# Storing the turned queries, keys and values of the head attention as the transposes yield them

## The chip, the core and the metric

The kernel runs on one core of a Trainium2 chip. The metric is the time of one execution on the device, in microseconds (us). The core's engines run side by side, each with its own queue of instructions, and meet through semaphores: PE (TensorE, the matrix products), DVE (VectorE), ACT (ScalarE), POOL (GpSimd) and SP (which here only issues DMA transfers). PEld is the loading of weights into PE, which overlaps with its products.

## The reference, cut to what matters

For each of 32 sequences of 256 tokens with 256 features, a linear ("performer") attention over a context runs first. Its result is added to `x`, and then a block with its own norms follows: an attention among the heads of each single token, and eight experts.

```python
x = x + tanh(g_xattn[0]) * xattn(layernorm(x), ctx_1024, ctx_1024, random_features)
x = x + tanh(g_ffn[0]) * ffn(layernorm(x), ...)

def ffn(x, ...):                                    # H = 16 heads of HD = 16 features
    h = rmsnorm(x, gamma1)
    q = (h @ Wq + bq).reshape(b, t, H, HD)
    kv = ((h @ Wdown + bdown) @ Wup + bup).reshape(b, t, H, 2 * HD)
    k, v = split(kv, 2, axis=-1)
    att = softmax(einsum('bthd,btgd->bthg', q, k) / sqrt(HD), axis=-1)
    out = einsum('bthg,btgd->bthd', att, v).reshape(b, t, D)
    x = x + (out @ Wo + bo)
    h2 = rmsnorm(x, gamma2)
    gate = softmax(h2 @ Wg + bg, axis=-1)
    return x + einsum('btd,edf,bte->btf', h2, We, gate)
```

The change concerns `q`, `k` and `v` of that attention among heads.

## The kernel before

One batch is one sequence: 256 tokens, as two tiles of 128 partitions by 256 features. Every engine has its list of steps; a step (`v_bd_`, `m00_`, `av0_`) is a small function that takes a batch number, waits for the steps that it needs, issues its instructions and signals its end. The order of the steps is written out by hand in each engine's part. A prologue brings in the first batches step by step, then a loop runs the function `slot(n)` 25 times (n = 6 to 30), and an epilogue drains the last batches. One slot works on several batches at once: features of the linear attention for batch n + 2, its scores and sums for n + 1, the norm of the second block for n, the head attention for n - 1, its output product for n - 2, the experts for n - 3.

The head attention of a batch goes like this. `bqq_`, `bkv0_` and `bkv1_` on DVE write queries, keys and values with their biases into `qkv`, tokens on the partitions. `q_t_`, `k_t_` and `v_t_` (lines 1519, 1612, 1581) turn blocks of 32 x 32 on DVE, so that the 16 features of a head lie on partitions and the tokens along the free side: `q_t` and `k_t` hold 32 tokens (n) by 16 heads, `v_t` 32 tokens by 16 features. Each of these tiles is stored with the token outside and the 16 inside, while the transpose yields 16 runs of 32 tokens; its destination is therefore written with a stride of 16 elements. Then the tiles are spread to block-diagonal operands: on ACT `q_bd_` makes two copies of `q_t` (line 899) and `k_bd_` four of `k_t` (line 932), each times a 0/1 column; on POOL `v_bd_` makes four of `v_t` (line 465). PE's `s_` multiplies `k_bd` with `q_bd` in 32 small products, DVE and ACT do the softmax, and PE's `pv_` multiplies the weights with `v_bd`.

Two other chains matter for the order. PE's `o_` (the product with `Wo`) for batch n - 2 is followed by `y2_` on DVE (line 1576), and that by `z0_` on POOL (lines 449 and 451). And the linear attention for batch n + 1 has masks on POOL: ACT copies scores to `att` (`x000_`, `x001_`, `x010_`, `x011_`), POOL blanks the future tokens (`m01_` line 473, `m00_` line 482), and PE's `av0_` (line 2348) multiplies with them. In POOL's slot these stand as `z0_(n - 2)`, `x1_(n)`, `v_bd_(n - 1)`, `m01_(n + 1)`, `m00_(n + 1)`. In PE's slot, `o_` stands ahead of six groups of score products (`X00_` to `X10_`), then come `av0_(n + 1)`, `s_(n - 1)`, `av1_(n + 1)`, `mm00_`, `mm01_`. Another POOL step, `d_v_` (line 420), copies 256 elements into `down_v`, reading every fourth.

Of the kernel before, what the change touches and what calls it, by code (L numbers as in the profile page):

```python
# [79 lines left out]
def build(nc, x_d, ctx_d, gx_d, gf_d, rf_d, g1_d, wq_d, bq_d, wdn_d, bdn_d, wup_d, bup_d,  # L80
          wo_d, bo_d, g2_d, wg_d, bg_d, we_d, out_d):
    ctx = ExitStack()
    with ctx:
# [57 lines left out]
        q_t, k_t, v_t = sb("q_t", [P, 32, H]), sb("k_t", [P, 32, H]), sb("v_t", [P, 32, HD])  # L141
# [33 lines left out]
        with ExitStack() as early:  # L175
# [18 lines left out]
            signal("once_pe0", "first_turned first_all most_turned stab_all"),  # L194
            signal("pe0", "fk fq X00 Y1"),
            signal("pe1", "X01 X11 av3 nt_t"),
            signal("pe2", "Y0 X10"),
            signal("pe3", "av0 av1"),
            signal("pe4", "hn_t qq s"),
            signal("pe5", "dn kv0"),  # L200
            signal("pe6", "kv1 pv"),
            signal("pe7", "o_tr o h2_t0"),
            signal("pe8", "h2_t1 mm1g mm10 mm11"),
            signal("pe9", "mm0g mm12"),
            signal("pe10", "mm00 mm01 mm03"),
            signal("pe11", "mm02 mm13"),
# [17 lines left out]
            signal("once_act0", "alpha we_hi3 wg_hi"),  # L224
            signal("keys_act0", "square"),
            signal("act0", "h_hi"),
            signal("act1", "k_hi h_t ek2"),
            signal("act2", "xn ek3 eq3"),
            signal("act3", "ek0 x000 x001 x100"),
            signal("act4", "q_hi eq0 x010"),  # L230
            signal("act5", "ek1 eq2 x011 x110 x101"),
            signal("act6", "eq1 nt0 nt1"),
            signal("act7", "x111"),
            signal("act8", "hn ht_hi d_hi q_bd"),
            signal("act9", "k_bd p_bd ot_hi"),
            signal("act10", "y"),
            signal("act11", "sq h2n h2_hi1"),
            signal("act12", "h2_hi0 gexp"),
            signal("once_pool0", "one_tri zero_id ident f_scale f_hi f_lo"),
            signal("pool0", "k_lo pk2"),  # L240
            signal("pool1", "rstd q_r"),
            signal("pool2", "q_lo pk0 m01 m10 m11"),
            signal("pool3", "pq3 m00"),
            signal("pool4", "v1"),
            signal("pool5", "pq1"),
            signal("pool6", "x1 r_f g_r"),
            signal("pool7", "d_v v_bd"),
            signal("pool8", "yb"),
            signal("pool9", "o_n ms_e r2"),
            signal("pool10", "z_y z0"),  # L250
# [41 lines left out]
        def _(sp):  # L292
            @per_batch
            def store_(b):
                if b >= 0:
                    sp.wait_ge(*at("a03", b))
                sp.wait_ge(*at("a13", b))
                sp.dma_start(rows(out_d, b), z[b % 2][:, :, :]).then_inc(*store.up(b))
# [91 lines left out]
            for n in range(6, NB + -1):  # L390
                slot(n)
# [6 lines left out]
            sp.wait_ge(*store.at(NB - 1))  # L398

        @block.gpsimd  # L400
        def _(pool):
# [6 lines left out]
            def pk0_(b):  # L408
                if b >= 0:
                    pool.wait_ge(*at("ek0", b))  # L410
# [43 lines left out]
            def x1_(b):  # L454
                if b >= 0:
# [21 lines left out]
            def m00_(b):  # L477
                if b >= 0:
                    pool.wait_ge(*at("x000", b))
                if b >= 0:  # L480
# [5 lines left out]
            def k_lo_(b):  # L486
                if b >= 0:
# [4 lines left out]
            def g_r_(b):  # L492
                pool.wait_ge(*at("g_bn", b))
                if b:
# [9 lines left out]
            def yb_(b):  # L504
                if b >= 0:
# [4 lines left out]
            def m10_(b):  # L510
                if b >= 0:
                    pool.wait_ge(*at("x100", b))
                pool.wait_ge(*at("x110", b))
# [21 lines left out]
            def m11_(b):  # L535
                if b >= 0:
                    pool.wait_ge(*at("x101", b))
                if b >= 0:
# [33 lines left out]
            def pk3_(b):  # L572
                if not b:
                    pool.wait_ge(*at("alpha"))
                if b >= 0:
# [239 lines left out]
            for n in range(6, NB + -1):  # L815
                slot(n)
# [15 lines left out]
            z0_(31)  # L832

        @block.scalar
        def _(act):
# [43 lines left out]
            def h_hi_(b):  # L879
                if b >= 1:  # L880
# [8 lines left out]
            def eq3_(b):  # L889
                if b >= 0:  # L890
# [4 lines left out]
            def q_bd_(b):  # L895
                if b >= 0:
# [6 lines left out]
            def k_hi_(b):  # L903
                if b >= 0:
# [18 lines left out]
            def x011_(b):  # L923
                if b >= 0:
# [11 lines left out]
            def y_(b):  # L936
                if b >= 1:
# [13 lines left out]
            def x110_(b):  # L951
                if b == 1:
                    act.wait_ge(*at("X11", b))
                if b >= 0:
# [4 lines left out]
            def h_t_(b):  # L959
                if b >= 0:  # L960
# [23 lines left out]
            def x101_(b):  # L984
                if b >= 0:
# [9 lines left out]
            def x111_(b):  # L995
                if b == 3:
                    act.wait_ge(*at("X11", b))
                if b >= 0:
# [4 lines left out]
            def sq_(b):  # L1003
                if b >= 0:
# [34 lines left out]
            def ek3_(b):  # L1039
                if b >= 0:  # L1040
# [9 lines left out]
            def ek1_(b):  # L1050
                if b >= 0:
# [337 lines left out]
            for n in range(6, NB + -1):  # L1389
# [34 lines left out]

        @block.vector
        def _(dve):
# [59 lines left out]
            def a13_(b):  # L1486
                if b >= 0:
                    dve.wait_ge(*at("a12", b))
                dve.wait_ge(*at("mm13", b))
# [19 lines left out]
            def h_tr_(b):  # L1509
                if b >= 0:  # L1510
                    dve.wait_ge(*at("h_lo", b))
                if b >= 1:
# [4 lines left out]
            def q_t_(b):  # L1517
                dve.wait_ge(*at("bqq", b))
                dve.transpose(q_t[:, :, :].rearrange("p n h -> p h n"), qkv[:, :, 0:D].rearrange("p t (h d) -> p h t d", d=HD)).then_inc(*up("q_t", b))

            @per_batch
            def ga_(b):
                dve.wait_ge(*at("mm0g", b))
                if b >= 0:
# [47 lines left out]
            def y2_(b):  # L1572
                dve.wait_ge(*at("o", b))
                if b >= 0:
# [4 lines left out]
            def v_t_(b):  # L1579
                dve.wait_ge(*at("bkv1", b))  # L1580
                dve.transpose(v_t[:, :, :].rearrange("p n d -> p d n"), qkv[:, :, 2 * D:3 * D].rearrange("p t (d g) -> p d t g", d=HD)).then_inc(*up("v_t", b))  # L1581

            @per_batch
            def a0g_(b):
                if b >= 0:
                    dve.wait_ge(*at("gate", b))
                if b >= 0:
# [19 lines left out]
            def k_t_(b):  # L1607
                if b >= 0:
                    dve.wait_ge(*at("bkv0", b))
                if b >= 0:  # L1610
                    dve.wait_ge(*at("bkv1", b))
                dve.transpose(k_t[:, :, :].rearrange("p n g -> p g n"), qkv[:, :, D:2 * D].rearrange("p t (g d) -> p g t d", d=HD)).then_inc(*up("k_t", b))  # L1612
# [1427 lines left out]
```

## Time and profile before

| what | value |
|---|---|
| median of 3 runs | 1070.0 us (1068.78 to 1070.27) |
| span of the profiled execution, first to last instruction | 1067.6 us |
| PE / PEld busy | 1012.6 us (95%) / 831.4 us (78%) |
| DVE busy | 961.4 us (90%) |
| ACT busy | 758.7 us (71%) |
| POOL busy | 752.5 us (70%) |
| chain that ended last | PE 87%, DVE 5%, POOL 4% |

For the profiled execution the span is the only time that the profile gives; the median of the runs lies 2.4 us above it. Busy time is the time in which an engine executes; waiting is not in it. Matmuls are pipelined and their ends are modelled, so a PE that is shown as busy throughout can still hold short waits. An idle time in brackets is that of the engine just before the instruction, with what ended it.

### The profile page before, as it was taken

The numbers are of one execution on the slowest core, as the hardware profiler recorded it, in microseconds if no ns is written. First come the engines' busy times: TensorE is split into PE (matmuls) and PEld (weight loads), VectorE is DVE, ScalarE is ACT, GpSimd is POOL, SyncE is SP. The second block draws the span as 40 slices with busy tenths as digits, with TensorE's granted clock in tenths as the row PEclk, the third lists the DMA queues.
The fourth block names the chain that finished last, engine by engine and source line by source line (L and its number), as shares of the span: only waits on it lengthen the run. The fifth ranks groups of instructions, "written<-read, shape, count | busy, mean of one in ns | idle before, by whom it ended". The sixth has DMA issues, their size and how long they took to land.

```text
span 1067.6 us, 32201 instructions
## 1 busy us (share of the span) xinstructions
PE 1012.6 (95%) x12870; PEld 831.4 (78%) x12870; DVE 961.4 (90%) x2176; ACT 758.7 (71%) x1564; POOL 752.5 (70%) x1111
## 2 busy tenths in 40 slices
PE   1568999999999999999999999999999999999998
PEld 0447788788888888888888888888888888888787
DVE  7778888999999999999999999999999999998996
ACT  6678877776677777668777666877766687776541
POOL 4578877787677778767778766777876677787531
PEclk9989999999999999999999999999999999999999
DMA  9501000011000001100100100010111000000000
GB/s 311 169 21 31 12 24 29 31 31 31 23 28 25 22 31 31 32 21 24 29 22 32 32 31 22 21 32 21 32 32 31 22 22 31 22 21 12 12 11 30
DMA packets 38915, 38.67 MB, mean 36 GB/s; under 512 B 3440, under 2 KB 38512, under 8 KB 38768
## 3 DMA queue, kind: packets, MB, share of 16 engines
q1 hardware_dynamic: 38384, 36.59, 10.9%
q8 instruction: 103, 1.69, 0.6%
q14 instruction: 44, 0.36, 0.1%
q0 software_dynamic: 384, 0.04, 0.0%
HBM read 28.23 MB, written 8.39 MB: 34 GB/s over the span
## 4 chain that ended last, share of the span: by engine, by line
PE 87%; DVE 5%; POOL 4%; issue 1%; ACT 1%; DMA 0%; SPq 0%; POOLq 0%; DVEq 0%; ACTq 0%
PE ps L2302 15%; PE ps L2304 14%; PE ps L2303 14%; PE ps L2333 10%; PE ps L2348 9%; PE ps L2341 5%; PE ps L2317 5%; PE ps L2382 3%; PE ps L2373 3%; PE ps L2296 2%; PE ps L2358 2%; DVE hk L1770 2%; PE ps L2366 1%; PE ps L2367 1%; PE ps L2325 1%
## 5 line engine op out<-in xcount | busy, mean ns | idle before, releaser
L1434 DVE SCALAR_TENSOR_TENSOR z<-ps,gate,z 128x256 f32<-128x256 f32 x512 | 238.5, 472 | 37.9 <-PE ps L2304 29.0
L2302 PE MATMUL ps<-we_hi,h_hi 128*128 128x512 f32 (+2 forms) x640 | 240.5, 376 | 0.6 <-DVE z L1434 0.4
L2304 PE MATMUL ps<-we_hi,h_lo 128*128 128x512 f32 (+2 forms) x640 | 224.1, 350 | 0.0
L2303 PE MATMUL ps<-we_lo,h_hi 128*128 128x512 f32 (+2 forms) x640 | 223.7, 349 | 0.0
L2302 PEld LDWEIGHTS ps<-we_hi,h_hi 128*128 128x128 f32 x640 | 120.4, 188 | 36.7 <-issue 12.6
L2333 PE MATMUL ps<-qf,kf 64*128 64x256 f32 x1024 | 129.2, 391 | 9.1 <-POOL kf L549 4.5
L2304 PEld LDWEIGHTS ps<-we_hi,h_lo 128*128 128x128 f32 x640 | 120.2, 188 | 17.1
L2303 PEld LDWEIGHTS ps<-we_lo,h_hi 128*128 128x128 f32 x640 | 120.8, 189 | 11.5
L2333 PEld LDWEIGHTS ps<-qf,kf 64*128 64x128 f32 x1024 | 96.4, 191 | 29.8 <-issue 11.3
L2348 PE MATMUL ps<-att,v 128*32 128x256 f32 (+1 forms) x2048 | 109.0, 329 | 3.1 <-POOL att L540 0.9
L911 ACT ACTIVATE att<-ps 128x512 f32<-128x512 f32 x32 | 19.1, 597 | 116.8 <-PE ps L2333 116.7
L2348 PEld LDWEIGHTS ps<-att,v 128*32 128x32 f32 x2048 | 57.4, 109 | 48.8 <-POOL att L482 11.8
L465 POOL TENSOR_SCALAR v_bd<-v_t,sel_blk 128x512 f32<-128x512 f32 x128 | 88.4, 713 | 6.3 <-DVE v_t L1581 6.3
L932 ACT ACTIVATE k_bd<-k_t,sel_blk 128x512 f32<-128x512 f32 x128 | 82.2, 733 | 2.9 <-DVE k_t L1612 2.9
L2341 PEld LDWEIGHTS ps<-qf,kf 64*128 64x128 f32 x1024 | 61.3, 190 | 9.5 <-ACT att L911 6.4
L2341 PE MATMUL ps<-qf,kf 64*128 64x128 f32 x1024 | 67.7, 281 | 0.9 <-POOL qf L442 0.9
L555 POOL TENSOR_TENSOR q_lo<-x_raw,q_hi 128x512 fp32r<-128x512 f32 x32 | 41.3, 1290 | 30.0 <-ACT q_hi L1047 30.0
L547 POOL TENSOR_SCALAR kf<-kf 128x512 f32<-128x512 f32 x31 | 19.1, 617 | 58.2 <-ACT kf L1032 57.7
L568 POOL TENSOR_TENSOR o_n<-o_tok,s_rec 128x512 f32<-128x512 f32 x32 | 41.6, 1301 | 13.7 <-DVE s_rec L1744 12.2
L530 POOL TENSOR_SCALAR ms_e<-ms 128x2 f32<-128x2 f32 x32 | 6.1, 191 | 60.6 <-ACT h2n L1007 60.2
L459 POOL TENSOR_TENSOR x<-o_x,x_in 128x512 f32<-128x512 f32 x32 | 40.8, 1274 | 4.5 <-POOL z L451 0.4
L489 POOL TENSOR_TENSOR k_lo<-c_raw,k_hi 128x512 fp32r<-128x512 f32 x32 | 41.6, 1299 | 2.4 <-ACT k_hi L906 2.1
(232 smaller groups left out, 3079.7 us busy)
## 6 DMA issues: line engine op xcount, KB each, us to landing
x_in<-in_x SPq DMA_DIRECT2D x32, 256.0 KB, 2.6
c_in<-in_ctx SPq DMA_DIRECT2D x32, 256.0 KB, 2.6
out<-z SPq DMA_DIRECT2D x32, 256.0 KB, 2.2
c_chunk<-in_ctx SPq DMA_DIRECT2D x14, 512.0 KB, 8.0
stage<-in_L_ffn_We SPq DMA_DIRECT2D x2, 1024.0 KB, 10.0
c_chunk<-in_ctx SPq DMA_DIRECT2D x2, 256.0 KB, 6.5
stage_b<-in_L_ffn_bup SPq DMA_DIRECT2D x1, 256.0 KB, 6.9
stage_q<-in_L_ffn_Wq SPq DMA_DIRECT2D x1, 256.0 KB, 6.4
```

What stands on the lines that cost most here:

```text
L465: last = pool.tensor_scalar(v_bd[:, :, a, 0:HD], v_t[:, :, :], sel_blk[:, a:a + 1], 1.0, ALU.mult, ALU.mult)
L489: pool.tensor_tensor(k_lo[:, :], c_raw[:, :], k_hi[:, :].bitcast(F32), ALU.subtract).then_inc(*up("k_lo", b))
L568: pool.tensor_tensor(o_n[:, :, :].rearrange("p t (h d) -> p d t h", d=HD), o_tok[:, 0:HD, :, :], s_rec[:, :, :].unsqueeze(1).to_broadcast( ...
L932: last = act.activation(k_bd[:, :, a, :], k_t[:, :, :], ACT.Copy, scale=sel_blk[:, a:a + 1])
L1434: return dve.scalar_tensor_tensor(out=z[b % 2][:, t, :], in0=ps[:, bank, offset:offset + D], scalar=gate[:, t, ex:ex + 1], in1=z[b % 2][:, ...
L2302: pe.matmul(out, a_hi(c), b_hi(c), start=(c == 0), stop=False)
L2303: pe.matmul(out, a_hi(c), b_lo(c), start=False, stop=False)
L2304: last = pe.matmul(out, a_lo(c), b_hi(c), start=False, stop=(c == C - 1))
L2317: last = pe.matmul(ps[:, BANK[f"f{of}{j}"], :], weight[own, :], src[own, :], start=(n == 0), stop=(n == 2 and not more), tile_position=(32 ...
L2333: last = pe.matmul(ps[:, banks[half], j * L:(j + 1) * L], kf[r, pr, 0:P], qf[r, pr, :], start=True, stop=True)
L2341: last = pe.matmul(ps[:, banks[half], j * P:(j + 1) * P], kf[r, pr, P:L], qf[r, pr, P:L], start=True, stop=True)
L2348: last = pe.matmul(ps[32 * j:32 * j + 32, bank, half * L + part * P:half * L + L], v1[:, part, 8 * oct + 2 * j + half, :], att[:, half, j, ...
```

## The change

The three tiles `q_t`, `k_t`, `v_t` are stored with the 16 outside and the 32 tokens inside, as the transposes yield them. The transposes then write their 512 elements one after the other. `q_bd_`, `k_bd_` on ACT and `v_bd_` on POOL read the tiles through a view that puts the token outside again, so that each element read lies 32 elements from the last, with 16 of them in a run. What they write has the same layout as before.

The conditions on many waits change too: waits taken for every batch (`if b >= 0`) are taken for a few batches only, where nothing else already implies them, and in some steps the order of two waits is exchanged. The order of the steps is the same on every engine. The banks and the buffers are the same; the list of signals is written in another order.

```diff
-        q_t, k_t, v_t = sb("q_t", [P, 32, H]), sb("k_t", [P, 32, H]), sb("v_t", [P, 32, HD])
+        q_t, k_t, v_t = sb("q_t", [P, H, 32]), sb("k_t", [P, H, 32]), sb("v_t", [P, HD, 32])
...
             def v_bd_(b):
                 pool.wait_ge(*at("v_t", b))
                 for a in range(4):
-                    last = pool.tensor_scalar(v_bd[:, :, a, 0:HD], v_t[:, :, :], sel_blk[:, a:a + 1], 1.0, ALU.mult, ALU.mult)
+                    last = pool.tensor_scalar(v_bd[:, :, a, 0:HD], v_t[:, :, :].rearrange("p d n -> p n d"), sel_blk[:, a:a + 1], 1.0, ALU.mult, ALU.mult)
...
             def m01_(b):
-                if b >= 0:
+                pool.wait_ge(*at("x011", b))
+                if b in (0, 2, 3, 4, 5):
                     pool.wait_ge(*at("x001", b))
-                pool.wait_ge(*at("x011", b))
...
             def m00_(b):
-                if b >= 0:
+                if b in (2, 3, 5):
                     pool.wait_ge(*at("x000", b))
-                if b >= 0:
+                if b in (0, 4, 6):
                     pool.wait_ge(*at("x010", b))
...
             def q_bd_(b):
-                if b >= 0:
+                if b in (0, 1, 2, 3, 31):
                     act.wait_ge(*at("q_t", b))
                 for t in range(T):
-                    last = act.activation(q_bd[:, :, t, :], q_t[:, :, :], ACT.Copy, scale=sel_tok[:, t:t + 1])
+                    last = act.activation(q_bd[:, :, t, :], q_t[:, :, :].rearrange("p h n -> p n h"), ACT.Copy, scale=sel_tok[:, t:t + 1])
...
                 for a in range(4):
-                    last = act.activation(k_bd[:, :, a, :], k_t[:, :, :], ACT.Copy, scale=sel_blk[:, a:a + 1])
+                    last = act.activation(k_bd[:, :, a, :], k_t[:, :, :].rearrange("p g n -> p n g"), ACT.Copy, scale=sel_blk[:, a:a + 1])
...
-                dve.transpose(q_t[:, :, :].rearrange("p n h -> p h n"), qkv[:, :, 0:D].rearrange("p t (h d) -> p h t d", d=HD)).then_inc(*up("q_t", b))
+                dve.transpose(q_t[:, :, :], qkv[:, :, 0:D].rearrange("p t (h d) -> p h t d", d=HD)).then_inc(*up("q_t", b))
...
-                dve.transpose(v_t[:, :, :].rearrange("p n d -> p d n"), qkv[:, :, 2 * D:3 * D].rearrange("p t (d g) -> p d t g", d=HD)).then_inc(*up("v_t", b))
+                dve.transpose(v_t[:, :, :], qkv[:, :, 2 * D:3 * D].rearrange("p t (d g) -> p d t g", d=HD)).then_inc(*up("v_t", b))
...
-                dve.transpose(k_t[:, :, :].rearrange("p n g -> p g n"), qkv[:, :, D:2 * D].rearrange("p t (g d) -> p g t d", d=HD)).then_inc(*up("k_t", b))
+                dve.transpose(k_t[:, :, :], qkv[:, :, D:2 * D].rearrange("p t (g d) -> p g t d", d=HD)).then_inc(*up("k_t", b))
...
             def mm01_(b):
-                if b >= 0:
+                if b >= 28:
                     pe.wait_ge(*at("a0g", b))
-                if b >= 1 and b + 4 < NB:
+                if 1 <= b < NB - 4:
                     pe.wait_ge(*at("nt0", b + 4))
...
```

## Rows read from the trace of the kernel before

**Rows 1.** The page, part 1: busy us (share of span) xinstructions.
```profile
span 1067.6 us, 32201 instructions
...
PE 1012.6 (95%) x12870; PEld 831.4 (78%) x12870; DVE 961.4 (90%) x2176; ACT 758.7 (71%) x1564; POOL 752.5 (70%) x1111
```

**Rows 2.** Busy us of each engine by stretch: stretch, its length, engines, clock, DMA.
```profile
80.00:120.00 40.00, 35.35 (x634) 28.15 (x633) 33.61 (x65) 36.45 (x74) 34.75 (x55) 1.00 0.10 29
...
600.00:700.00 100.00, 99.94 (x1262) 82.52 (x1262) 93.09 (x210) 70.95 (x149) 74.47 (x109) 1.00 0.09 29
```

**Rows 3.** Timeline of one slot, PE: start, us, instruction; then DVE's `y2_`.
```profile
600.13 0.28 PE L2304 MATMUL ps<-wo_hi,ot_lo 128*128 128x256 f32 x1
...
606.85 1.90 PE L2333 MATMUL ps<-qf,kf 64*128 64x256 f32 x16
608.76 0.86 PE L2348 MATMUL ps<-att,v 128*32 128x256 f32 x16
609.47 1.10 PE L2373 MATMUL ps<-k_bd,q_bd 128*32 128x64 f32 x64
...
600.45 0.69 DVE L1576 TENSOR_TENSOR y<-ps,y 128x512 f32<-128x512 f32 x1
```

**Rows 4.** Timeline of the same slot, POOL, from `z0_` to `m00_`.
```profile
601.31 0.69 POOL L449 TENSOR_SCALAR z<-y,tanh_f 128x512 f32<-128x512 f32 x1 [1.04 <-DVE y L1576]
602.09 1.28 POOL L451 TENSOR_TENSOR z<-z,x 128x512 f32<-128x512 f32 x1
603.51 1.27 POOL L459 TENSOR_TENSOR x<-o_x,x_in 128x512 f32<-128x512 f32 x1
604.76 2.77 POOL L465 TENSOR_SCALAR v_bd<-v_t,sel_blk 128x512 f32<-128x512 f32 x4
607.47 0.65 POOL L473 TENSOR_SCALAR_AFFINE_SELECT att<-att 128x512 f32<-128x512 f32 x1
608.06 0.64 POOL L482 TENSOR_SCALAR_AFFINE_SELECT att<-att 128x512 f32<-128x512 f32 x1
```

**Rows 5.** The view of `m00_`'s line, who waited for it: us in all, times.
```profile
  PEld ps L2348: 11.8, 28
```

**Rows 6.** Groups by line, DVE: count | busy us, mean ns | idle before.
```profile
L1519 DVE STREAM_TRANSPOSE q_t<-qkv 128x512 f32<-128x512 f32 x32 | 34.2, 1069 | 0.0
...
L1734 DVE STREAM_TRANSPOSE x_raw<-xn 128x512 f32<-128x512 f32 x32 | 22.4, 699 | 0.3 <-ACT xn L1014 0.3
...
L1449 DVE STREAM_TRANSPOSE c_raw<-c_in 128x512 f32<-128x512 f32 x32 | 21.2, 662 | 0.0
```

**Rows 7.** The chain that ended last, between 60 and 135 us: start, us, what.
```profile
101.49 1.12 DVE k_t L1612
...
114.10 2.14 POOL v_bd L465 x4
...
116.79 0.64 POOL att L514
```

**Rows 8.** Groups by line, POOL: `v_bd_`, `d_v_`, a plain copy, a plain cast.
```profile
L465 POOL TENSOR_SCALAR v_bd<-v_t,sel_blk 128x512 f32<-128x512 f32 x128 | 88.4, 713 | 6.3 <-DVE v_t L1581 6.3
...
L420 POOL CAST down_v<-down 128x256 fp32r<-128x256 f32 x32 | 20.5, 640 | 15.1 <-DVE down L1505 13.4
...
L436 POOL COPY v<-c_in 128x512 f32<-128x512 f32 x32 | 19.7, 617 | 3.7 <-PE ps L2348 2.0
...
L609 POOL CAST f_hi<-stage_f 128x128 fp32r<-128x128 f32 x1 | 0.3, 289 | 0.1
```

**Rows 9.** Timeline of the same slot, ACT: the long idle time, and `k_bd_`.
```profile
604.31 0.60 ACT L911 ACTIVATE att<-ps 128x512 f32<-128x512 f32 x1 [4.38 <-PE ps L2333]
...
606.23 2.57 ACT L932 ACTIVATE k_bd<-k_t,sel_blk 128x512 f32<-128x512 f32 x4
```

**Rows 10.** Timeline of the same slot, PE: the end of `mm00_`, the start of `mm01_`.
```profile
612.42 0.40 PE L2304 MATMUL ps<-we_hi,h_lo 128*128 128x512 f32 x1
612.65 0.40 PE L2302 MATMUL ps<-we_hi,h_hi 128*128 128x512 f32 x1
```

More of the change, by code:

```diff
@@ L193, in build @@
         signals = [
[L194 to L206, printed above, removed]
+            signal("once_pool0", "one_tri zero_id ident f_scale f_hi f_lo"),
+            signal("pool0", "k_lo pk2"),
+            signal("pool1", "rstd q_r"),
+            signal("pool2", "q_lo pk0 m01 m10 m11"),
+            signal("pool3", "pq3 m00"),
+            signal("pool4", "v1"),
+            signal("pool5", "pq1"),
+            signal("pool6", "x1 r_f g_r"),
+            signal("pool7", "d_v v_bd"),
+            signal("pool8", "yb"),
+            signal("pool9", "o_n ms_e r2"),
+            signal("pool10", "z_y z0"),
+            signal("keys_act0", "square"),
+            signal("once_act0", "alpha we_hi3 wg_hi"),
+            signal("act0", "h_hi"),
+            signal("act1", "k_hi h_t ek2"),
+            signal("act2", "xn ek3 eq3"),
+            signal("act3", "ek0 x000 x001 x100"),
+            signal("act4", "q_hi eq0 x010"),
+            signal("act5", "ek1 eq2 x011 x110 x101"),
+            signal("act6", "eq1 nt0 nt1"),
+            signal("act7", "x111"),
+            signal("act8", "hn ht_hi d_hi q_bd"),
+            signal("act9", "k_bd p_bd ot_hi"),
+            signal("act10", "y"),
+            signal("act11", "sq h2n h2_hi1"),
+            signal("act12", "h2_hi0 gexp"),
             signal("once_dve0", "zero_f first_least first_most first less_first least_ least stabilizer kept gamma2 less"),
@@ L223, in build @@
             signal("dve14", "a03"),
[L224 to L250, printed above, removed]
+            signal("once_pe0", "first_turned first_all most_turned stab_all"),
+            signal("pe0", "fk fq X00 Y1"),
+            signal("pe1", "X01 X11 av3 nt_t"),
+            signal("pe2", "Y0 X10"),
+            signal("pe3", "av0 av1"),
+            signal("pe4", "hn_t qq s"),
+            signal("pe5", "dn kv0"),
+            signal("pe6", "kv1 pv"),
+            signal("pe7", "o_tr o h2_t0"),
+            signal("pe8", "h2_t1 mm1g mm10 mm11"),
+            signal("pe9", "mm0g mm12"),
+            signal("pe10", "mm00 mm01 mm03"),
+            signal("pe11", "mm02 mm13"),
         ]
@@ L389, in _ @@
             load_c_(8)
-            for n in range(6, NB + -1):
+            for n in range(6, NB - 1):
                 slot(n)
@@ L814, in _ @@
             pk3_(7)
-            for n in range(6, NB + -1):
+            for n in range(6, NB - 1):
                 slot(n)
@@ L1388, in _ @@
             ek3_(7)
-            for n in range(6, NB + -1):
+            for n in range(6, NB - 1):
                 slot(n)
@@ L2191, in _ @@
             ht_lo_(5)
-            for n in range(6, NB + -1):
+            for n in range(6, NB - 1):
                 slot(n)
@@ L2414, in mm13_ @@
             def mm13_(b):
-                if b >= 0:
+                if b in (1, 30):
                     pe.wait_ge(*at("a02", b))
-                if not b or b == NB - 1 or 2 <= b < NB - 2:
+                if b in (0, 31) or 2 <= b < NB - 2:
                     pe.wait_ge(*at("a03", b))
@@ L2461, in o_tr_ @@
             def o_tr_(b):
[L2462 removed]
+                pe.wait_ge(*at("o_n", b))
+                if b in (0, 2) or 4 <= b < NB - 3:
                     pe.wait_ge(*at("eq2", b + 3))
[L2464 removed]
                 turn(ps[:, BANK["otr"], :], o_n).then_inc(*up("o_tr", b))
@@ L2947, in _ @@
             qq_(5)
-            for n in range(6, NB + -1):
+            for n in range(6, NB - 1):
                 slot(n)
```

204 lines of the change are left out of this document (101 added, 103 removed).

## The prediction

> **What bounds the kernel now.** Busy shares come first: PE 95%, DVE 90%, ACT 71%, POOL 70% [rows 1]. Shares over the whole span mix stages, so the second view is the busy time by stretch [rows 2]. Between 600 and 700 us PE is busy 99.94 us of 100 and DVE 93 of 100; between 80 and 120 us, while the pipeline over the batches fills, PE is still idle for 4.7 us of 40. Read quickly, this says that PE sets the pace for some 800 us and that POOL and ACT have a quarter of every slot to spare. A busy PE is only modelled, though, so the third view is the timeline of one slot around the head attention [rows 3, 4]. The walk to follow there is on POOL. The output product `o_` ends on PE at 600.13 + 0.28 = 600.41. `y2_` on DVE starts on it at 600.45 and takes 0.69. POOL starts `z0_` at 601.31 and from there never stops: `z0_` (0.69 and 1.28), `x1_` (1.27), the four instructions of `v_bd_` (2.77 together), `m01_` (0.65), `m00_` from 608.06 to 608.70. PE's `av0_` starts at 608.76, 0.06 us after `m00_`, and the view of `m00_`'s line says who waited for it: PE's weight load for `att`, in 28 of 32 batches, 11.8 us in all or 0.42 each [rows 5]. So PE already waits in nearly every slot for a mask that stands behind `v_bd_` in POOL's queue. `v_bd_`'s own reader, `pv_`, comes long after; the instruction is critical not for its result but for its place.
>
> **The transposes on DVE: faster, and nearly free of effect.** The three transposes of 512 elements with a strided destination take about 1070 ns (`q_t_` 1069); those of the same size with a plain one take 662 (`c_t_`) and 699 (`x_t_`) [rows 6]. I take 690 for the new ones, 0.38 us less each, 1.14 us a batch, 36 us of DVE's busy time in all. In the loop DVE is not what PE waits for. The place where it might help is the start of POOL's walk: `q_t_` stands ahead of `y2_` on DVE. But `y2_` starts 0.04 us after `o_` has ended on PE, and cannot start sooner however early DVE is free. So nothing in the 25 loop slots. In the fill one of these transposes is on the chain that ended last, `k_t_` of batch 1 at 101.49 [rows 7]; 15 fall into the fill, 5.7 us in all; I take 2 us. In the drain there are six, 2.3 us in all; I take 0.5.
>
> **`v_bd_` on POOL: the price of the new read.** Before, its four instructions read `v_t` front to back, 713 ns each. Now every element read lies 32 elements (128 bytes) from the last. The trace has one POOL instruction that reads with a stride, `d_v_`, which takes every fourth element: 640 ns for 256 elements. What 256 elements should cost without a stride comes from two plain reads, a cast of 128 elements (289 ns, the same operation and output type) and a copy of 512 (617 ns; it writes in runs of 16 as `v_bd_` does): (617 - 289) / 384 = 0.854 ns an element, so 289 + 128 x 0.854 = 398 ns [rows 8]. The stride costs 640 - 398 = 242 ns, or 0.945 ns an element. On 512 elements that is 484 ns, and on four instructions 1.94 us a slot. From below the price is nothing, if only that one form is slow; from above I take 0.55 us each, 2.2 us a slot, an estimate from the same row with some 15% more for the eightfold step. I take 1.94, since `d_v_` is the only strided read on this engine.
>
> The Trainium skill has a rule against this change: "GPSIMD Engine Reference", section "Performance pitfalls for Q7 kernels", says that a read from SBUF with a step over 8 bytes costs about 2.9 cycles an element where 1.9 would do. One cycle at the 1.2 GHz of its section "Specifications" would be 0.83 ns, 427 ns an instruction and, as an estimate, 1.71 us a slot and 43 us in 25 slots. By that rule `d_v_` (a step of 16 bytes) pays too, and the trace agrees: 242 ns on 256 elements.
>
> **Where that lands.** `m01_` and `m00_` follow `v_bd_` on POOL without a gap, and PE waits for `m00_` already. All 1.94 us go to PE, in each of the 25 loop slots (n = 6 to 30): 48.5 us. It cannot be won back inside the slot: POOL's walk begins with the end of `o_`, which PE's own order sets. In the fill `v_bd_` stands ahead of masks too, for batches 0 to 4. For batch 1 it is itself on the chain (114.10), with a mask behind it [rows 7]. The bounds are 0 and 5 x 1.94 = 9.7 us; I take 6, as PE is not yet fully loaded there. In the drain no mask stands behind `v_bd_`: 0.
>
> **`q_bd_` and `k_bd_` on ACT: a price that is covered.** Six instructions a batch read with the same stride of 32. No ACT row of this trace reads SBUF with a stride, so the bounds are nothing and POOL's 0.48 us each. `q_bd_` is followed, after one more instruction, by 4.38 us in which ACT waits for PE [rows 9]; it is covered in full. `k_bd_` takes 2.57 us and ends at 608.80; its reader `s_` starts on PE at 609.47, 0.67 later. If it grows by 4 x 0.48 = 1.9 us, it ends at 610.7, while `s_`, standing behind the late `av0_`, starts at 609.47 + 1.94 = 611.4. So with POOL slow, ACT's growth costs nothing in the loop. Without POOL's delay it would cost 1.9 - 0.67 = 1.25 us a slot (a rival, below).
>
> **The waits that go.** Orders are the same on every engine, but many waits that were taken for every batch are now taken for a few, and some pairs change places. Separate wait instructions fall from 751 to 329 on PE, from 448 to 130 on DVE, from 225 to 76 on POOL. A wait that is already met costs little: `mm01_` has two before, and starts at 612.65, 0.23 us after the matmul ahead of it, the pitch inside a group [rows 10]; `m01_` has two, and starts before `v_bd_` has ended [rows 4]. Bounds 0 and -4 us (0.15 in each loop slot, an estimate that is below any gap in these rows); I take -1.
>
> **The sum.** +48.5 (loop) + 6 (fill, POOL) - 2 (fill, DVE) - 0.5 (drain) - 1 (waits) = +51 us. The profiled execution spans 1067.6 us and the median of the runs shown is 1070.0, 2.4 above it; taking these as unchanged, 1067.6 + 51 + 2.4 = **1121 us**.
>
> **Rivals.**
> - *POOL doesn't mind the stride* (chance 0.12). For it: `d_v_` is another operation with another pattern. Against it: nothing else in that row explains 242 ns. Then the loop stays as it is, and what remains is the gain in fill and drain and on waits, 0.5 to 7 us: about 1066 us, the faster side. It decides below 0.03 us of growth an instruction; above that, four of them in 25 slots (3 us) use up the gain.
> - *POOL doesn't mind, ACT does* (0.04). `k_bd_` then outruns its 0.67 us of cover: 25 x 1.25 = 31 us, about 1099.
> - *POOL is slower but the mask has room* (0.03), as its 70% busy share and PE's 99.9% suggest: about 1070. The wait in 28 batches speaks against it.
> - *Both are slower than I allow* (0.03), so that `k_bd_` grows past 2.6 us and delays `s_` as well: above 1136.
>
> My forecast has the rest, 0.78, between 1100 and 1136: from below with 0.35 us an instruction in 25 slots (35 us) and 5 less from fill and waits, from above with 2.2 us a slot (55) and 9 from the fill. The range, with the ACT rival in it, is 1096 to 1136. A change of 0.2% (2 us) is about the least that a measurement of this kernel can tell. Faster: most of the first rival, 0.11. Same: the third and the rest of the first, 0.04. Slower: 0.85.
>
> **What would show it.** In the profile after: the three transposes at 660 to 710 ns; `v_bd_` at about 1200 ns (right) or near 713 (the first rival); the wait for `m00_`'s line up from 0.42 to some 2.3 us a batch; in PE's busy time by stretch 92 to 94 us of 100 instead of 99.9; `k_bd_` anywhere between 733 and 1220 ns without effect. The forecast falls if `v_bd_` stays below 800 ns, or if `m00_` ends as late as I say and `av0_` does not wait.

## The result, and the profile after

The kernel after takes **1130.5 us** (median of 4 runs, 1130.39 to 1131.75) beside 1069.8 for the kernel before on the same chip: a ratio of 1.0572, 95% interval 1.0557 to 1.0587. That is 61 us slower; the forecast was 51 us, with a range of 1096 to 1136. Its profiled execution spans 1128.7 us.

The page's part 1 of the kernel after (busy us, share of the span, instructions), to be read beside [rows 1]:
```profile
span 1128.7 us, 31279 instructions
...
PE 1017.1 (90%) x12870; PEld 833.3 (74%) x12870; DVE 954.4 (85%) x2176; ACT 850.6 (75%) x1564; POOL 812.2 (72%) x1111
```
PE works about as long as before (1012.6); it now stands still for 112 us instead of 55. ACT has 92 us more to do and POOL 60, yet neither is busy for more than some 75% of the span. The shares alone would not say where the time went.

The groups by line after, for five of the six edited lines (count | busy us, mean ns of one | idle before, and what ended it), beside [rows 6], [rows 8] and the ACT lines of the same kind:
```profile
L466 POOL TENSOR_SCALAR v_bd<-v_t,sel_blk 128x512 f32<-128x512 f32 x128 | 147.5, 1177 | 5.8 <-DVE v_t L1584 5.8
...
L934 ACT ACTIVATE k_bd<-k_t,sel_blk 128x512 f32<-128x512 f32 x128 | 143.7, 1220 | 1.8 <-DVE k_t L1615 1.7
...
L901 ACT ACTIVATE q_bd<-q_t,sel_tok 128x512 f32<-128x512 f32 x64 | 76.7, 1251 | 0.0
...
L1615 DVE STREAM_TRANSPOSE k_t<-qkv 128x512 f32<-128x512 f32 x32 | 22.5, 702 | 0.1
...
L1522 DVE STREAM_TRANSPOSE q_t<-qkv 128x512 f32<-128x512 f32 x32 | 21.7, 678 | 0.0
```
`v_bd_` grew from 713 to 1177 ns, `k_bd_` from 733 to 1220. The transposes fell from about 1070 to between 678 and 702 (`v_t_` 699).

Busy us by stretch, kernel after, with the columns of [rows 2]:
```profile
600.00:700.00 100.00, 94.79 (x1221) 78.61 (x1220) 88.01 (x202) 79.06 (x147) 76.13 (x104) 1.00 0.08 26
80.00:120.00 40.00, 32.87 (x511) 25.75 (x511) 26.95 (x56) 35.24 (x60) 31.12 (x45) 0.96 0.10 28
```
The same walk as in [rows 3, 4], one slot of the kernel after (start, us, instruction, idle time before it): the end of `o_` on PE, `y2_` on DVE, POOL from `z0_` to `m00_`, ACT's `k_bd_`, then PE's `av0_` and `s_`.
```profile
633.96 0.28 PE L2308 MATMUL ps<-wo_hi,ot_lo 128*128 128x256 f32 x1
...
634.28 0.69 DVE L1579 TENSOR_TENSOR y<-ps,y 128x512 f32<-128x512 f32 x1
...
635.07 0.69 POOL L450 TENSOR_SCALAR z<-y,tanh_f 128x512 f32<-128x512 f32 x1 [0.96 <-DVE y L1579]
...
638.47 4.61 POOL L466 TENSOR_SCALAR v_bd<-v_t,sel_blk 128x512 f32<-128x512 f32 x4
...
640.07 4.47 ACT L934 ACTIVATE k_bd<-k_t,sel_blk 128x512 f32<-128x512 f32 x4
...
643.63 0.63 POOL L483 TENSOR_SCALAR_AFFINE_SELECT att<-att 128x512 f32<-128x512 f32 x1
...
644.31 0.86 PE L2352 MATMUL ps<-att,v 128*32 128x256 f32 x16 [1.73 <-POOL att L483]
...
644.98 1.08 PE L2377 MATMUL ps<-k_bd,q_bd 128*32 128x64 f32 x64
```
From the end of `o_` (634.24) to the end of `m00_` (644.26) it is now 10.02 us; before it was 608.70 - 600.41 = 8.29. `v_bd_` grew from 2.77 to 4.61 in the middle of it, and PE stands for 1.73 us until the mask is there. `k_bd_` ends at 644.54, still 0.44 before `s_` begins.

The view of `m00_`'s line in the kernel after, who waited for it (us, times), beside [rows 5]:
```profile
  PEld ps L2352: 54.6, 29
  PE ps L2352: 43.4, 25
```
Before, it was nearly always the weight load alone that waited, 0.42 us each; now it waits 1.88 each, and the matmuls themselves 1.74.

### The profile page after: what moved, and what is told of

It is laid out like the page before. It is cut to its first block, busy times and chain, and to the rows that moved or that the text cites. A ratio compares the mean times of both kernels' runs of the same rounds, so it can differ in the third digit from the quotient of the medians.

```text
span 1128.7 us, 31279 instructions
## 1 busy us (share of the span) xinstructions
PE 1017.1 (90%) x12870; PEld 833.3 (74%) x12870; DVE 954.4 (85%) x2176; ACT 850.6 (75%) x1564; POOL 812.2 (72%) x1111
## 4 chain that ended last, share of the span: by engine, by line
PE 52%; POOL 25%; DVE 13%; ACT 5%; issue 2%; DMA 2%; SPq 1%; POOLq 0%; DVEq 0%
POOL v_bd L466 12%; PE ps L2306 10%; PE ps L2308 9%; PE ps L2307 8%; PE ps L2352 8%; PE ps L2321 4%; POOL x L460 3%; POOL z L452 3%; PE ps L2386 3%; ACT k_bd L934 2%; PE ps L2377 2%; PE ps L2362 2%; DVE z L1437 2%; POOL z L450 2%; DVE y L1579 2%
## 5 line engine op out<-in xcount | busy, mean ns | idle before, releaser
L466 POOL TENSOR_SCALAR v_bd<-v_t,sel_blk 128x512 f32<-128x512 f32 x128 | 147.5, 1177 | 5.8 <-DVE v_t L1584 5.8
L934 ACT ACTIVATE k_bd<-k_t,sel_blk 128x512 f32<-128x512 f32 x128 | 143.7, 1220 | 1.8 <-DVE k_t L1615 1.7
L901 ACT ACTIVATE q_bd<-q_t,sel_tok 128x512 f32<-128x512 f32 x64 | 76.7, 1251 | 0.0
```

What stands on the lines that cost most here:

```text
L466: last = pool.tensor_scalar(v_bd[:, :, a, 0:HD], v_t[:, :, :].rearrange("p d n -> p n d"), sel_blk[:, a:a + 1], 1.0, ALU.mult, ALU.mult)
L901: last = act.activation(q_bd[:, :, t, :], q_t[:, :, :].rearrange("p h n -> p n h"), ACT.Copy, scale=sel_tok[:, t:t + 1])
L934: last = act.activation(k_bd[:, :, a, :], k_t[:, :, :].rearrange("p g n -> p n g"), ACT.Copy, scale=sel_blk[:, a:a + 1])
```

## The experiments

To split a span in parts, the start of `s_` on PE is taken as a mark (L2377 in the kernel after). PE's timeline of the kernel after, `s_` of batches 5, 9 and 29:
```profile
251.16 1.08 PE L2377 MATMUL ps<-k_bd,q_bd 128*32 128x64 f32 x64
...
382.45 1.08 PE L2377 MATMUL ps<-k_bd,q_bd 128*32 128x64 f32 x64
...
1038.67 1.08 PE L2377 MATMUL ps<-k_bd,q_bd 128*32 128x64 f32 x64
```
A slot is (1038.67 - 382.45) / 20 = 32.81 us. The fill is what lies ahead of batch 5's `s_`, the loop the 24 slots from there to batch 29's, the drain the rest. Read the same way in each profiled execution:

| kernel | median us | ratio (95%) | slot | fill | loop | drain |
|---|---|---|---|---|---|---|
| before | 1069.8 | 1 | 31.22 | 234.7 | 749.3 | 83.6 |
| after | 1130.5 | 1.0572 (1.0557–1.0587) | 32.81 | 251.2 | 787.5 | 90.0 |
| e1_waits_only | 1064.6 | 0.9950 (0.9936–0.9965) | 31.01 | 234.0 | 744.3 | 83.1 |
| e2_v_only | 1119.1 | 1.0465 (1.0446–1.0484) | 32.88 | 245.9 | 789.1 | 83.1 |
| e3_qk_only | 1124.1 | 1.0506 (1.0489–1.0524) | 32.72 | 247.8 | 785.2 | 89.4 |
| e4_no_reorder | 1064.5 | 0.9950 (0.9935–0.9965) | 31.03 | 235.0 | 744.7 | 83.0 |
| e5_v_only_late | 1157.8 | 1.0829 (1.0810–1.0848) | 34.50 | 245.1 | 829.0 | 84.8 |
| e6_waits_v_late | 1097.7 | 1.0267 (1.0250–1.0284) | 32.39 | 233.5 | 777.3 | 83.2 |
| e7_write_strided | 1120.5 | 1.0480 (1.0465–1.0496) | 32.63 | 249.5 | 783.1 | 86.2 |
| e8_q_only | 1069.7 | 1.0004 (0.9995–1.0014) | 31.02 | 239.2 | 744.5 | 84.8 |
| e9_v_only_split | 1087.4 | 1.0150 (1.0124–1.0176) | 31.46 | 242.4 | 754.9 | 83.2 |
| e10_waits_split | 1074.0 | 1.0041 (1.0027–1.0055) | 31.41 | 235.4 | 753.9 | 83.0 |
| e11_after_split | 1138.9 | 1.0642 (1.0626–1.0658) | 33.20 | 251.1 | 796.6 | 88.6 |
| e12_waits_split2 | 1064.3 | 0.9948 (0.9934–0.9961) | 31.03 | 234.6 | 744.7 | 83.1 |

### e1_waits_only: the new waits, the old layout

From the kernel after, the layout of all three arrays, their transposes and their readers go back; `k_t` and `q_t` likewise:
```diff
-dve.transpose(v_t[:, :, :], qkv[...])
+dve.transpose(v_t[:, :, :].rearrange("p n d -> p d n"), qkv[...])
...
-last = pool.tensor_scalar(v_bd[:, :, a, 0:HD], v_t[:, :, :].rearrange("p d n -> p n d"), ...)
+last = pool.tensor_scalar(v_bd[:, :, a, 0:HD], v_t[:, :, :], ...)
```


> The changed kernel with the three tiles, their transposes and their readers as before; only the waits are those of the change. Theory: waits that are already met cost almost nothing, 1067 to 1070 us, period of a loop slot 31.1 to 31.2 us as before. Rival: the some 420 fewer separate waits on PE are worth real time, 1060 to 1065 us, and hid a part of the layout's price in the comparison.

It takes 1064.6 us, 5.2 less than before. So the waits are worth five times what the prediction gave them, and the layout alone costs 1130.5 - 1064.6 = 66 us. POOL's timeline of one slot of e1 shows one part, beside [rows 4]:
```profile
598.05 0.70 POOL L450 TENSOR_SCALAR z<-y,tanh_f 128x512 f32<-128x512 f32 x1 [0.93 <-DVE y L1579]
598.83 1.29 POOL L452 TENSOR_TENSOR z<-z,x 128x512 f32<-128x512 f32 x1
600.21 1.27 POOL L460 TENSOR_TENSOR x<-o_x,x_in 128x512 f32<-128x512 f32 x1
...
604.76 0.64 POOL L483 TENSOR_SCALAR_AFFINE_SELECT att<-att 128x512 f32<-128x512 f32 x1
```
`z0_` starts after 0.93 us of idle time instead of 1.04, and `x1_` 0.09 us after the instruction ahead of it instead of 0.14. Each of these steps had a second wait that was met long before. With `o_` ending at 597.23, the walk to the end of `m00_` (605.40) is 8.17 us instead of 8.29. The slot is shorter by 0.21 us. The start times of PE's instructions, as the mean of 19 slots, show where: 0.10 lies at the mask, where the time from the start of the last matmul of `X10_` to the first of `av0_` falls from 0.41 to 0.31 us, and most of the rest ahead of the key features (line 2321, 0.05) and of `s_` (0.03), on PE, which has 422 wait instructions fewer. In the stretch from 600 to 700 us PE is busy 100.00 of 100 in e1.

### e2_v_only and e3_qk_only: each engine's part alone

e2 is e1 with the new layout for `v_t` alone (POOL's part); e3 is e1 with it for `q_t` and `k_t` (ACT's part). From the kernel after, e3 is:
```diff
-q_t, k_t, v_t = sb("q_t", [P, H, 32]), sb("k_t", [P, H, 32]), sb("v_t", [P, HD, 32])
+q_t, k_t, v_t = sb("q_t", [P, H, 32]), sb("k_t", [P, H, 32]), sb("v_t", [P, 32, H])
```
and the transpose and the reader of `v_t` as in e1.

> The changed kernel with queries and keys stored and read as before; only the values keep the new layout, so only v_bd_ on GpSimd reads with a stride. Theory: the loop's loss is all v_bd_'s (slot period 32.8 us, +40 us in 25 slots), while a good part of the 21 us outside the loop is ScalarE's: 1112 to 1120 us. Rival: ScalarE's growth is covered everywhere, in fill and drain too: 1128 to 1132 us, as the changed kernel.

> The changed kernel with the values stored and read as before; only queries and keys keep the new layout, so only q_bd_ and k_bd_ on ScalarE read with a stride. Theory: without GpSimd's delay k_bd_ outruns its cover of 0.67 us: four instructions of +0.49 us less 0.67 are 1.28 us in each of 25 slots, 32 us, and some 8 to 15 us more in fill and drain: 1107 to 1117 us. Rival 1: ScalarE stays covered, 1066 to 1075 us. Rival 2: the other engines shift so that only part of it comes through, 1080 to 1100 us.

Each alone costs nearly as much as both: 1119.1, and 1124.1, which is more than the theory of e3 allowed. The waits of PE in e2, then in e3 (who waits for whom: us in all, times, longest):
```profile
PE ps L2352 <- POOL att L483: 46.8, 26, 1.8
```
```profile
PE ps L2377 <- ACT k_bd L934: 33.4, 26, 2.2
...
PE ps L2306 <- ACT att L958: 4.9, 25, 0.2
```
In e2 PE waits in 26 batches for `m00_`, behind `v_bd_`, 1.80 us each. In e3 it waits in 26 for `k_bd_`, 1.28 each, and a further 0.2 in `mm00_` for `x110_`, which stands behind `k_bd_` on ACT; by the start times on PE, the mean of 19 slots again, the two steps lose 1.43 and 0.27 us against e1. A slot is 1.86 us longer than e1's in e2, 1.70 in e3 and 1.80 in the kernel after. The two delays pass at the same time, so the slot pays the larger one and not the sum. Outside the loop they add in part: against e1 the fill is longer by 11.9, 13.8 and 17.2 us, the drain by 0, 6.3 and 6.9.

### e4_no_reorder: the transposes alone

The readers take the stored array front to back; the rearrangement is left out, so the operands come out in another order:
```diff
-... v_t[:, :, :].rearrange("p d n -> p n d"), ...
+... v_t[:, :, :].rearrange("p h n -> p (h n)").rearrange("p (a b) -> p a b", b=16), ...
```


> The changed kernel, but the readers on ScalarE and GpSimd read the tiles front to back, as stored, so that the operands are in the wrong order: the rearrangement is left out. It has the gain on VectorE (transposes of about 0.69 us) and none of the price. Theory: VectorE is not what the loop waits for: 1064 to 1069 us, slot period 31.1 to 31.2 us. Rival: the faster transposes let y2_ and so GpSimd's walk start sooner, slot period 30.8 us or less: 1055 to 1061 us.

1064.5 us, the same as e1. 36 us less of transposes on DVE are worth nothing, neither in the loop nor in fill or drain, and the whole loss of the change lies in the strided access.

### e8_q_only: the drain and the fill of `q_bd_`

e8 is e1 with the new layout for `q_t` alone.

> The changed kernel with keys and values stored and read as before; only the queries keep the new layout, so only q_bd_ (two instructions of 1.25 us for 0.71) is dearer. Theory: in the loop it is covered by ScalarE's idle time ahead of the score copies (slot period 31.0 us), in fill and drain it is not: 1066 to 1072 us against 1064.6 of e1. Rival: covered everywhere, 1064 to 1065 us; or on the loop's path, 1085 us or more.

`q_bd_` is covered in the loop (a slot of 31.02 us, e1's 31.01), as the prediction said, but not outside it: the fill is 5.2 us longer than e1's and the drain 1.7. The price of the two `q_bd_` instructions, 1.07 us a batch, uses up what the waits give.

### e7_write_strided: the stride on the other side

The readers walk the stored array in its order and write with the stride:
```diff
-last = pool.tensor_scalar(v_bd[:, :, a, 0:HD], v_t[:, :, :].rearrange("p d n -> p n d"), ...)
+last = pool.tensor_scalar(v_bd[:, :, a, 0:HD].rearrange("p n d -> p d n"), v_t[:, :, :], ...)
```


> The changed kernel, but the readers walk in the stored order: they read front to back and write with the stride (64 to 272 bytes) instead. Theory: GpSimd's price is one of reading (its o_n_ writes with a step of 64 bytes at the price of its plain two-operand instructions), so v_bd_ returns to some 710 ns; ScalarE has no such row in the trace of before, and is taken as GpSimd: 1063 to 1068 us. Rival 1: the stride costs on either side, 1125 to 1132 us. Rival 2: GpSimd writes freely and ScalarE does not, 1118 to 1126 us as in e3.

Groups by line of e7:
```profile
L466 POOL TENSOR_SCALAR v_bd<-v_t,sel_blk 128x512 f32<-128x512 f32 x128 | 144.1, 1227 | 5.8 <-DVE v_t L1584 5.8
L934 ACT ACTIVATE k_bd<-k_t,sel_blk 128x512 f32<-128x512 f32 x128 | 130.9, 1196 | 1.7 <-DVE k_t L1615 1.7
...
L901 ACT ACTIVATE q_bd<-q_t,sel_tok 128x512 f32<-128x512 f32 x64 | 72.4, 1243 | 0.0
```
1227, 1196 and 1243 ns beside 1177, 1220 and 1251 with the strided read: to write with a stride costs POOL and ACT about as much as to read with one. That only reading is dear did not hold. By busy time, in which overlapping neighbours count once, the four copies of `k_bd_` are somewhat cheaper than in the kernel after, 130.9 / 32 = 4.09 us instead of 143.7 / 32 = 4.49, and those of `v_bd_` take 4.50 instead of 4.61; e7 as a whole is 10 us shorter.

### e5_v_only_late and e6_waits_v_late: `v_bd_` behind the masks

If only the place ahead of the masks costs, `v_bd_` behind them should be free. e5 is e2, e6 is e1, both with
```diff
-v_bd_(n - 1)
 m01_(n + 1)
 m00_(n + 1)
+v_bd_(n - 1)
 k_lo_(n + 2)
 g_r_(n)
```


> The kernel of e2 (only the values in the new layout) with v_bd_ moved behind the two masks m01_ and m00_ in GpSimd's slot; the fill is left as it is. The price of v_bd_ stays (1177 ns each), its place changes. Theory (the place costs, not the busy time): slot period back to 30.8 to 31.0 us, the 55 us of e2 shrink to the fill's 9 to 12: 1070 to 1077 us. Rival (GpSimd's added 1.86 us a slot costs wherever it stands): 1112 to 1120 us as in e2.

> The kernel of e1 (old layout, new waits) with v_bd_ behind the two masks in the loop. Theory: in e1 PE still waits about 0.2 to 0.3 us a slot for m00_, which now ends 2.8 us sooner: slot period 30.75 to 30.85 us, 1058 to 1061 us, faster than both kernels. Rival: another step ends last at once (y00_, or the copies on ScalarE), and nothing is gained: 1064 to 1065 us.

Both are slower than their partners, e6 by 33 us, e5 by 39, and slower than any rival had it. e6's timeline of POOL, then its waits (who waits for whom: us in all, times, longest):
```profile
619.18 0.64 POOL L474 TENSOR_SCALAR_AFFINE_SELECT att<-att 128x512 f32<-128x512 f32 x1 [1.79 <-ACT att L928]
```
```profile
POOL att L474 <- ACT att L928: 45.5, 26, 1.8
ACT hn L975 <- POOL shift_f L502: 38.5, 26, 1.5
...
PE ps L2321 <- ACT att L1002: 17.0, 24, 0.7
PE ps L2300 <- ACT hn L975: 11.1, 26, 1.0
```
The masks cannot run sooner than ACT has copied the scores, so POOL now waits 1.79 us that `v_bd_` had filled. Then `v_bd_` delays `g_r_`, ACT's `hn_` waits for `g_r_`, and PE's `hn_t_` for `hn_`, 0.43 us each. PE waits longer still, 0.71 us each, in the key features for the copy `x111_` (line 1002), which stands behind `hn_` on ACT. In e5, with the slow `v_bd_`, the same view has for the wait of `hn_t_`:
```profile
PE ps L2300 <- ACT hn L975: 50.7, 27, 2.0
```
This stretch of POOL has two deadlines, the mask's and `g_r_`'s, and moving all of `v_bd_` over the first one breaks the second.

### e9_v_only_split, e10_waits_split, e11_after_split: `v_bd_` in two pieces

One copy (e9, e11) or two (e10) stay ahead of the masks; the rest goes behind `q_r_`, and `yb_` behind `m11_`. `pv_` and `y2_` take back their wait in every batch.
```diff
 v_bd_(n - 1)
 m01_(n + 1)
 m00_(n + 1)
 k_lo_(n + 2)
 g_r_(n)
-yb_(n - 1)
 m10_(n + 1)
 q_r_(n + 2)
+v_bd_rest_(n - 1)
 r2_(n - 2)
 m11_(n + 1)
+yb_(n - 1)
```


> The kernel of e2 (only the values in the new layout, strided v_bd_ at 1177 ns) with another place for v_bd_ in GpSimd's loop slot: one of its four copies stands ahead of the masks m01_ and m00_, where GpSimd waits for ScalarE's score copies anyway (1.8 us a slot in e5), the other three behind k_lo_, g_r_, m10_ and q_r_, and yb_ behind m11_; pv_ and y2_ get their waits back. Theory (the queue has two deadlines, the masks for av0_ and g_r_ for hn_, and only what stands ahead of them costs): slot period 30.8 to 31.1 us, the fill's 6 to 12 us stay: 1066 to 1078 us. Rival (the added 1.86 us a slot costs in any place): 1112 us or more.

> The kernel of e1 (old layout, new waits) with the same order on GpSimd, two of the four copies ahead of the masks. Theory: PE's last 0.2 to 0.3 us of waiting for m00_ in each slot go, slot period 30.75 to 30.9 us: 1058 to 1063 us, faster than both kernels. Rival: another step ends last at once, 1064 to 1066 us; or a third deadline of that queue is missed, as in e6: slower than 1070 us.

> The changed kernel with the order of e9 on GpSimd. Theory: GpSimd's and ScalarE's delays run side by side, and the loop has the longer of both, so with GpSimd's gone ScalarE's k_bd_ holds the loop as in e3 (slot period 32.6 to 32.8 us): 1120 to 1130 us, next to nothing gained. Rival: the delays add, and GpSimd's share of the loop (some 40 us) goes: 1085 to 1095 us.

e9 keeps the slow instructions and wins back 32 of the 55 us by which e2 is longer than e1, by order alone: the slot falls from 32.88 to 31.46, and PE no longer waits for `m00_` in the loop. (The parts in the table are of a run 5 us below the median.) It keeps 8.4 us in the fill and 0.45 us a slot, and is 9 us above what the theory allowed. e10, with fast instructions, loses 0.40 us a slot too, so that rest is not the stride. One of PE's waits in e10, and DVE's and POOL's timeline, tell where it is:
```profile
PE ps L2389 <- DVE att L1662: 5.3, 24, 0.2
```
```profile
610.41 1.27 POOL L495 TENSOR_TENSOR k_lo<-c_raw,k_hi 128x512 fp32r<-128x512 f32 x1
610.60 1.11 DVE L1655 TENSOR_SCALAR var_f<-mvg 128x2 f32<-128x2 f32 x1
...
611.69 0.68 DVE L1662 TENSOR_TENSOR att<-ps,causal 128x512 f32<-128x512 f32 x1
```
`var_f` is a pair of DVE instructions of two elements. The first takes 1.11 us here and ends (611.71) just as POOL's `k_lo_` ends (611.68). `y01_` starts behind the pair, and `s_` on PE waits for `y01_`. In e1 the pair meets `m00_` on POOL instead; there the second is the long one:
```profile
604.65 0.18 DVE L1643 TENSOR_SCALAR var_f<-mvg 128x2 f32<-128x2 f32 x1
604.74 0.68 DVE L1644 TENSOR_SCALAR var_f<-mvg 128x2 f32<-128x2 f32 x1
```
It ends at 605.42, `m00_` at 605.40. e11 is the kernel after in e9's order: `m00_` holds PE no more, but `k_bd_` does. `var_f`'s first instruction takes 896 ns on the mean, as long as in e10 (892), and the slot is 0.39 longer than the kernel after's, e10's loss; that it is the same cause here was not isolated. It is 8 us slower than the kernel after, which neither its theory nor its rival had. PE's wait in e11:
```profile
PE ps L2389 <- ACT k_bd L947: 32.9, 26, 2.3
```

### e12_waits_split2: is it `k_lo_` that `var_f` waits for?

e10 with the two late copies ahead of `k_lo_`, so that a copy of 0.70 us and not `k_lo_` of 1.27 is under way when `var_f` comes:
```diff
 m00_(n + 1)
+v_bd_rest_(n - 1)
 k_lo_(n + 2)
 g_r_(n)
 m10_(n + 1)
 q_r_(n + 2)
-v_bd_rest_(n - 1)
 r2_(n - 2)
```


> The kernel of e10 with one change: the last two copies of v_bd_ stand right behind the masks and ahead of k_lo_, instead of behind q_r_. In e10 the small VectorE instruction that writes var_f took 1.1 us and ended with GpSimd's k_lo_ (1.3 us), where in e1 its second one ended with m00_; the copy y01_ behind it, for which PE's s_ waits, came 0.4 us later, and that is the whole loss of e10. Theory (a VectorE instruction of this form ends only with the GpSimd instruction that is under way): now a copy of 0.7 us is under way, var_f takes 0.5 us at most, y01_ starts 0.15 us sooner than in e1, the slot is PE's own again: slot period 30.95 to 31.05 us, 1062 to 1066 us. Rival: the loss of e10 came from the waits that were put back or from yb_'s new place: slot period 31.4 us, 1072 to 1076 us.

Groups by line, the first of the `var_f` pair in e10, then in e12:
```profile
L1655 DVE TENSOR_SCALAR var_f<-mvg 128x2 f32<-128x2 f32 x32 | 28.5, 892 | 1.1
```
```profile
L1655 DVE TENSOR_SCALAR var_f<-mvg 128x2 f32<-128x2 f32 x32 | 15.5, 485 | 1.1
```
It falls from 892 to 485 ns on the mean, the slot from 31.41 to 31.03 and the time by 9.7 us to 1064.3. POOL's `z0_` and `m00_` in one slot of e12:
```profile
598.88 0.70 POOL L450 TENSOR_SCALAR z<-y,tanh_f 128x512 f32<-128x512 f32 x1 [0.96 <-DVE y L1591]
...
604.68 0.64 POOL L488 TENSOR_SCALAR_AFFINE_SELECT att<-att 128x512 f32<-128x512 f32 x1
```
The mask is done 6.44 us after `z0_` starts, where e1 takes 605.40 - 598.05 = 7.35, and the slot is the same: with the new waits, `m00_` is no longer what the old layout waits for. e12 and e1 both beat the kernel before, by 0.5%; neither beats the other.

## Why the prediction held, step by step

- **The bound.** Right in what it led to. PE waits for `m00_` behind `v_bd_`, and e2 shows it: its four copies grow by (149.6 - 88.4) / 32 = 1.91 us, beside [rows 8], and its slot by 1.86 against e1; in the kernel after it is 1.85 and 1.80.
```profile
L466 POOL TENSOR_SCALAR v_bd<-v_t,sel_blk 128x512 f32<-128x512 f32 x128 | 149.6, 1199 | 5.8 <-DVE v_t L1584 5.8
```
All of it sits in one place on PE: from the start of the last matmul of `X10_` to the first of `av0_` it takes 2.18 us in e2 and 2.11 in the kernel after, 0.31 in e1. But the prediction read too much into the wait before. The 0.42 us are the weight load's, and `av0_` started 0.01 us after the end of `X10_` (606.85 + 1.90 = 608.75 [rows 3]). The mask cost PE some 0.10 us a slot, 0.41 instead of 0.31, and e12, with the mask done 0.9 us sooner than in e1, has 0.31 too. So the mask stood just at the edge, with nothing to spare, and that is enough for the whole growth to come through; the wait rose to 1.88 and not to the 2.3 forecast. That DVE and PE look busier and POOL looks free did not count. "POOL doesn't mind" and "the mask has room" fall with the same rows.
- **The price of the stride on POOL.** Right, from one row: 0.945 ns an element predicted from `d_v_`, (1177 - 713) / 512 = 0.906 measured. The Trainium skill ("GPSIMD Engine Reference", "Performance pitfalls for Q7 kernels") has one cycle more an element for such a read, 0.83 ns as an estimate; the trace lies between that and the forecast.
- **The loop.** Predicted 1.94 us a slot. Against e1, 24 slots are longer by 787.5 - 744.3 = 43.2 us, 1.80 each. The kernel after's slot is 0.07 shorter than e2's, in which ACT is fast; its four copies of `v_bd_` take 0.07 less (147.5 and 149.6 us in all), and why they do was not followed up.
- **ACT covered in the loop.** Right, but narrowly: 0.44 us are left between `k_bd_` and `s_`, since `k_bd_` came out at the upper bound (+0.487 us). Without POOL's delay it costs more than the 1.25 us of the rival "ACT alone": e3's slot is 1.70 longer than e1's. That rival had charged only `s_`'s wait for `k_bd_`; `mm00_` waits behind it as well.
- **The transposes.** The duration is right (678 to 702 ns, 690 predicted). The 2.5 us of gain in fill and drain are not there: e4 is e1.
- **The waits.** Mis-sized: 1 us predicted, bound 4, measured 5.2. The two starts that the prediction read were of steps where every wait was long met and nothing ahead was late. What costs is a met wait beside one that comes last: 0.05 to 0.11 us each in `z0_` and `x1_`, on the walk that the slot of the kernel before waited for, and so half of the 0.21 us a slot. The rest is on PE itself.
- **Fill and drain.** This is the step that failed: +3.5 us predicted, 17.2 + 6.9 = 24.1 measured against e1. One slot's growth, 1.80, has to come off, since batch 5's `s_` stands in slot 6, the first of the prediction's 25; that leaves 22.3. The larger part is ACT, which the prediction called covered from rows of a loop slot and did not price outside it; its rows in the fill and in the drain were not read. POOL alone (e2) costs 11.9 in the fill, 10.0 without slot 6, where 6 were taken and 9.7 was the bound. Some 3 of these 10 seem to go with the clock: e2's two runs with a mean granted clock of 0.997 took 1117.2 and 1118.3 us, the two with 0.992 took 1119.9 and 1122.0. In its profiled run, one of the latter, PE was busy for only 3.2 of the 5 us from 208 to 213, and then the granted clock fell to 0.50 for a while (the lower of its two levels, 1.2 and 2.4 GHz). Batch 5's `s_`, behind that, falls 5.4 us further behind e1's; in a later slot it is 1.9. The stretch from 200 to 220 us (columns of [rows 2]) in e1, then in e2:
```profile
200.00:220.00 20.00, 20.00 (x330) 15.81 (x327) 17.92 (x44) 15.06 (x31) 14.20 (x23) 1.00 0.13 42
```
```profile
200.00:220.00 20.00, 18.01 (x234) 13.20 (x236) 14.99 (x36) 14.04 (x27) 16.71 (x25) 0.91 0.08 27
```
So POOL's term was near, as far as these four runs tell, and ACT's was missing. The chain that ended last in the kernel after, in the fill, beside [rows 7], and in the drain (start, us, what):
```profile
107.94 4.45 ACT k_bd L934 x4
...
113.67 2.13 ACT q_bd L901 x2
...
120.66 4.58 POOL v_bd L466 x4
...
1059.64 2.29 ACT q_bd L901 x2
1061.93 4.48 ACT k_bd L934 x4
...
1079.50 4.64 ACT k_bd L934 x4
1084.14 2.12 ACT q_bd L901 x2
```
In the fill `k_bd_` and `v_bd_` of one batch stand on the chain one after the other, where a loop slot has them side by side. In the drain ACT's six instructions stand in a row, twice, with PE waiting; `v_bd_` costs nothing there, as predicted (e2's drain is e1's). A part of it is the clock here too: from 80 to 120 us the granted clock is 0.96 of the 2.4 GHz level where it was 1.00 [rows 2], and the mean over the span is 0.991 instead of e1's 0.997. What lowered it at 80 us is not shown; in the 20 us ahead PE was busy for 16.92, in e1 for 16.59. As an estimate from the two means the clock costs at most 0.009 x 1128.7 - 0.003 x 1061.4 = 7 us in all. No run held the clock fixed, so its share is not settled.

That the total came out near the forecast is in part luck, because the errors ran against each other: some 19 us too little in fill and drain, 3.5 too much in the loop (48.5 for 25 slots, 45.0 measured) and 4 to 5 too little gained on waits (45.0 + 22.3 - 6.2 = 61.1 in the spans).

## What to carry to other kernels

Price a slower instruction where it stands in its queue and not by its engine's share: follow what comes behind it until something waits, in the loop, and again, from other rows, in fill and drain, where steps that run side by side in the loop come one after the other. When an order is changed to make room, look for the second deadline of the stretch. A plain store that saves DVE 0.38 us is a bad bargain where four copies on POOL, or four on ACT, pay 0.5 us each for it, whichever side of the copy has the stride.

## What the hardware showed that was not expected

- **A tiny DVE instruction waits for POOL.** One `var_f` instruction (two elements in, two out) took 0.68 us in e1's slot and one 1.11 in e10's, where the other of the pair took 0.16 to 0.18; both long ones ended 0.02 to 0.03 us after the POOL instruction that was under way. The same holds for all of e10's 27 long ones, and for the 27 of e12, which end with the copy of `v_bd_`; e12 exchanged that POOL instruction and got the time back. The Trainium skill ("SBUF — State Buffer", "SBUF: two separate sides") says that VectorE and GpSimd share a pair of ports under an exclusive lock, which a VectorE instruction takes in a 2-port mode or with two SBUF inputs, and that the one who comes second waits for the whole instruction; the trace agrees with the wait, with the 0.02 us beside it, while the mode in which `var_f` runs is in no trace here.
- **The stride costs ACT as much as POOL**, 0.487 us (`k_bd_`) and 0.536 (`q_bd_`) for 512 elements, and most of that on the write too: the four copies of `k_bd_` take 2.57 us plain [rows 9], 4.49 with the strided read and 4.09 with the strided write.
- **Waits already met are not free**: 422 fewer on PE, 318 on DVE and 149 on POOL, with the steps in the same order, and some pairs exchanged, are worth 5.2 us of 1070.
